# A decoder layer on one core: the projection stage of its mixer written out pass by pass, with other loads, statistics and transposes in its order

## The reference

```python
def _layernorm(x, axis=-1, eps=1e-05):
    m = jnp.mean(x, axis=axis, keepdims=True)
    v = jnp.var(x, axis=axis, keepdims=True)
    return (x - m) / jnp.sqrt(v + eps)
...
proj = jnp.einsum('btd,od->bto', x, W_in)
gate = proj[..., :DI]
value_raw = proj[..., DI:2 * DI]
params = proj[..., 2 * DI:].reshape(Bsz, Tlen, H, 2)
xp = jnp.pad(value_raw, ((0, 0), (K - 1, 0), (0, 0)))
conv = dw_bias + sum((xp[:, k:k + Tlen, :] * dw_weight[:, k] for k in range(K)))
value = jax.nn.silu(conv)
```

## Time and profile before

| What | us |
|---|---|
| median of 3 runs | 3239.29 |
| the profiled execution | 3251.73 |
| its span, first to last instruction | 3249.9 |
| projections in it, start to the first instruction of the mixer stage | 269.7 |
| of these, start to the first transpose | 29.7 |
| start of the first to start of the last pass's transposes (29.68 to 226.91) | 197.2 |

### The profile page before, as it was taken

One profiled execution on the slowest core, in us unless ns is written; L12 is line 12 of the kernel. 1 busy time (PEld: TensorE's weight loads), 2 busy tenths in 40 slices (PEclk: granted clock), 3 DMA queues, 4 the chain that ended last, 5 costly groups with the idle time before them and its releaser, 6 DMA issues. The chain is left out here.

```text
span 3249.9 us, 83432 instructions
## 1 busy us (share of the span) xinstructions
PE 2870.0 (88%) x34208; PEld 2165.1 (67%) x34208; DVE 2067.0 (64%) x7109; ACT 1299.5 (40%) x2250; POOL 287.0 (9%) x227
## 2 busy tenths in 40 slices
PE   5885699999999999999999998698887399999996
PEld 2444587788778877787887887333344166888885
DVE  5444999999999998899999998455452000111110
ACT  3443445454554455455544553133331021333332
POOL 0000000000000000000000000000004600434343
PEclk9887799999999999999999998689988599999998
DMA  6566323543354325433543242200062201777777
GB/s 225 160 160 177 93 83 82 131 106 89 76 131 105 96 69 131 105 90 74 132 107 105 71 118 72 75 1 1 1 238 91 104 14 56 202 206 203 205 203 214
DMA packets 249371, 373.92 MB, mean 115 GB/s; under 512 B 54203, under 2 KB 172108, under 8 KB 238156
## 3 DMA queue, kind: packets, MB, share of 16 engines
q1 hardware_dynamic: 226572, 340.18, 37.9%
q0 software_dynamic: 22464, 28.95, 4.4%
HBM read 269.18 MB, written 104.04 MB: 115 GB/s over the span
## 5 line engine op out<-in xcount | busy, mean ns | idle before, releaser
L603 PE MATMUL ring<-valt,wbc 128*128 128x256 f32 x4096 | 947.1, 388 | 28.8 <-DMA valt<-valt_scratch 28.1
L603 PEld LDWEIGHTS ring<-valt,wbc 128*128 128x128 f32 x4096 | 777.7, 194 | 166.7 <-issue 58.9
L756 ACT COPY bc<-ring 128x512 f32<-128x512 f32 x256 | 149.8, 585 | 746.6 <-PE ring L603 746.6
L916 DVE TENSOR_TENSOR uu<-phi,coef 128x64 f32<-128x64 f32 x2048 | 367.1, 223 | 2.1
L922 DVE TENSOR_TENSOR phi<-phi,uu 128x64 f32<-128x64 f32 x2048 | 367.3, 223 | 0.0
L2039 DVE TENSOR_SCALAR f_yr<-fp_y,f_meta 128x256 f32<-128x256 f32 x124 | 54.3, 480 | 415.8 <-PE fp_y L1856 415.8
L661 PE MATMUL yp<-bc,hpad 32*32 32x64 f32 x8192 | 260.4, 289 | 5.2 <-DVE hc L1024 5.0
L661 PEld LDWEIGHTS yp<-bc,hpad 32*32 32x32 f32 x8192 | 225.5, 122 | 51.3 <-issue 51.2
L1923 ACT ACTIVATE f_hT<-fp_h,f_b 128x256 f32<-128x256 f32 x248 | 117.6, 474 | 327.7 <-PE fp_h L1847 327.7
L1856 PE MATMUL fp_y<-f_w,f_hT 128*128 128x256 f32 x992 | 230.7, 386 | 7.9
L1723 POOL DMA_INDIRECT acc_scratch<-f_yr,f_meta x124 | 192.6, 1553 | 445.5 <-DVE f_yr L2039 304.7
(11 more groups left out here) (227 smaller groups left out, 4102.2 us busy)
## 6 DMA issues: line engine op xcount, KB each, us to landing
f_w<-in_W_dram SPq DMA_DIRECT2D x128, 512.0 KB
coef<-par_scratch SPq DMA_DIRECT2D x128, 256.0 KB
fb<-fac_scratch SPq DMA_DIRECT2D x256, 128.0 KB, 3.3
fc<-fac_scratch SPq DMA_DIRECT2D x256, 128.0 KB, 4.0
xg_scratch<-f_fill SPq DMA_DIRECT2D x16, 1032.0 KB, 17.3
f_xr<-xg_scratch SPq DMA_DIRECT2D x64, 258.0 KB
vtok_scratch<-p_vtok SPq DMA_DIRECT2D x32, 512.0 KB, 7.0
dub<-vtok_scratch SPq DMA_DIRECT2D x16, 1024.0 KB, 7.8
```

Of the source, the lines that this page charges most:

```text
L603: mm = pe.matmul(ring[:, p % 2, v * UT:(v + 1) * UT], wbc[:, k, g, first + v, :], valt[:, u % 2, k, :], start=(k == 0), stop=(k == 3))
L756: nc.scalar.copy(bc[:, gp, first:first + 2, i // 2, :], o).then_inc(bc_ready, 1)
L916: made[k] = mark(V.tensor_tensor(uu[:, k].rearrange("p i (g b) -> p i g b", b=B), phi[:, t, ::-1, k, :].rearrange("p i (g b) -> p i g b", ...
```

## The change

The stage does the same arithmetic on the same sizes; the loop of 4 rounds becomes straight-line code, pass by pass, with waits for constants, and the order changes:

- x is loaded by 8 DMAs of one pass each (512 KB). The first is issued ahead of the weights, the others behind them and ahead of `wbc`.
- VectorE takes the statistics of the first pass's 4 tiles alone, norms them, and then takes those of the other 28 tiles.
- TensorE's order in a pass is val, par, vt of the pass before, xT of the next pass, gate. `xnt` has two buffers.
- ScalarE takes the next pass's `xnt` and the last pass's `vtok` in the same order; the silu of `cv` stays behind that of the gates.
- VectorE norms the next pass's tiles ahead of a pass's convolution, and waits for the silu of the pass before ahead of writing `cv`.
- SP stores raw, vtok of the pass before, sg, valt. The `stored` semaphores are split by what they guard.

```diff
-PRING = [("xT", 0), ("xT", 1)] + [("val", m) for m in range(4)] + [("par",)]
-PRING += [("gate", m) for m in range(4)] + [("vt", b) for b in range(B)]
+def projection_order():
+
+    order = [("xT", 0, k) for k in range(2)]
+    for u in range(NPASS):
+        order += [("val", u, m) for m in range(4)] + [("par", u, 0)]
+        if u > 0:
+            order += [("vt", u - 1, b) for b in range(B)]
+        if u + 1 < NPASS:
+            order += [("xT", u + 1, k) for k in range(2)]
+        order += [("gate", u, m) for m in range(4)]
+    return order + [("vt", NPASS - 1, b) for b in range(B)]
+
+
+PRING = projection_order()
...
-        xt = sb("xt", [P, NT, DM])
-        bst = sb("bst", [P, NT, 6])
-        mv = sb("mv", [P, NT, 2])
-        std = sb("std", [P, NT])
-        rstd = sb("rstd", [P, NT])
+        xt = sb("xt", [P, NPASS, PA, DM])
+        bst = sb("bst", [P, NPASS, PA, 6])
+        mv = sb("mv", [P, NPASS, PA, 2])
+        std = sb("std", [P, NPASS, PA])
+        rstd = sb("rstd", [P, NPASS, PA])
...
-        xnt = sb("xnt", [P, 2, PT])
+        xnt = sb("xnt", [P, 2, 2, PT])
...
+            xv = x.rearrange("(a u p) m -> u p a m", a=PA, p=P)
+            sp.dma_start(xt[:, 0], xv[0]).then_inc(x_first, 16)
...
+            for u in range(1, NPASS):
+                sp.dma_start(xt[:, u], xv[u]).then_inc(x_in, 16)
...
-                sg_ready.wait(sp, u, 4)
+                    sp.dma_start(st["raw"][q, u // 2, :, (u % 2) * PT:(u % 2 + 1) * PT],
+                                 rawp[q * H:(q + 1) * H, :]).then_inc(raw_out, 16)
+
+            def store_sg(u):
+                sp.wait_ge(sg_ready, 4 * u + 4)
                 for v in range(2):
-                    sp.dma_start(st["sg"][2 * u + v], sg[:, par, :, v * UT:(v + 1) * UT]).then_inc(stored[par].sem, 16)
-
-                vtok_ready.wait(sp, u, 4 * B)
+                    sp.dma_start(st["sg"][2 * u + v], sg[:, u % 2, :, v * UT:(v + 1) * UT]).then_inc(sg_out[u % 2], 16)
+
+            def store_valt(u):
+                sp.wait_ge(valt_ready, 4 * u + 4)
+                for v in range(2):
+                    sp.dma_start(st["valt"][2 * u + v], valt[:, u % 2, :, v * UT:(v + 1) * UT]) \
+                        .then_inc(valt_out[u % 2], 16)
+
+            def store_vtok(u):
+                sp.wait_ge(vtok_ready, 2 * B * (u + 1))
                 for v in range(2):
                     for q in range(2):
-                        sp.dma_start(st["vtok"][2 * u + v, q], vtok[v * L:(v + 1) * L, par, :, q, :]) \
-                            .then_inc(stored[par].sem, 16)
-                valt_ready.wait(sp, u, 4)
...
+            for u in range(NPASS):
+                store_raw(u)
+                if u > 0:
+                    store_vtok(u - 1)
+                store_sg(u)
+                store_valt(u)
+            store_vtok(NPASS - 1)
...
-                xn_ready.wait(pe, u, 1)
-
-                vtok_ready.wait(pe, u, 2 * B)
...
+            normed_turned(0)
+            for u in range(NPASS):
+                values(u)
+                if u > 0:
+                    values_turned(u - 1)
+                if u + 1 < NPASS:
+                    normed_turned(u + 1)
+                gates(u)
+            values_turned(NPASS - 1)
...
-            nc.scalar.activation(std[:], mv[:, :, 1], ACT.Sqrt, bias=epsln[:, 0:1]).then_inc(std_ready, 1)
-            act.wait_ge(w_loaded, 16 * NW)
...
+            nc.scalar.activation(std[:, 0], mv[:, 0, :, 1], ACT.Sqrt, bias=epsln[:, 0:1]).then_inc(std_ready, 1)
...
+            def values(u):
+                if u >= 2:
+                    act.wait_ge(conv_ready, 4 * (u - 1) + 4)
...
+                if u > 0:
+                    act.wait_ge(raw_out, 32 * u)
...
+            normed_turned(0)
+            for u in range(NPASS):
+                values(u)
+                if u == 0:
+                    act.wait_ge(stats_ready, 2)
+                    nc.scalar.activation(std[:, 1:].rearrange("p u a -> p (u a)"),
+                                         mv[:, 1:, :, 1].rearrange("p u a -> p (u a)"), ACT.Sqrt,
+                                         bias=epsln[:, 0:1]).then_inc(std_ready, 1)
+                else:
+                    values_turned(u - 1)
+                if u + 1 < NPASS:
+                    normed_turned(u + 1)
+                gates(u)
+                convolved(u)
+            values_turned(NPASS - 1)
...
-            dve.wait_ge(x_in, 16)
-            for n in range(NT):
-                ins = V.bn_stats(bst[:, n, :], xt[:, n, :])
-            ins.then_inc(step, 1)
-            dve.wait_ge(step, 1)
-            for n in range(NT):
-                ins = V.bn_aggr(mv[:, n, :], bst[:, n, :])
-            ins.then_inc(stats_ready, 1)
-            dve.wait_ge(std_ready, 1)
-            V.reciprocal(rstd[:], std[:]).then_inc(step, 1)
-            dve.wait_ge(step, 2)
-            dve.wait_ge(w_loaded, 16 * NW)
...
+            def statistics(u0, u1, k):
+                for u in range(u0, u1):
+                    for a in range(PA):
+                        ins = V.bn_stats(bst[:, u, a, :], xt[:, u, a, :])
+                link(ins)
+                for u in range(u0, u1):
+                    for a in range(PA):
+                        ins = V.bn_aggr(mv[:, u, a, :], bst[:, u, a, :])
+                ins.then_inc(stats_ready, 1)
+                dve.wait_ge(std_ready, k)
+                link(V.reciprocal(rstd[:, u0:u1], std[:, u0:u1]))
...
+            def normed(u):
+                if u >= 2:
+                    dve.wait_ge(xnt_ready, 2 * (u - 1))
...
+                    if u > 0:
+                        dve.wait_ge(valt_ready, 4 * (u - 1) + k + 1)
...
+            dve.wait_ge(x_first, 16)
+            statistics(0, 1, 1)
+            normed(0)
+            dve.wait_ge(x_in, 16 * (NPASS - 1))
+            statistics(1, NPASS, 2)
+            dve.wait_ge(w_loaded, 16 * NW)
+            for u in range(NPASS):
+                if u + 1 < NPASS:
+                    normed(u + 1)
+                convolution(u)
```

More of the change, by code:

```diff
@@ L121, in projections @@
         std_ready = sem("std_ready")
[L122 to L132, removed]
-        step = sem("step")
[L135 to L144, removed]
+        ring_full = sem("ring_full")
+        xn_ready = sem("xn_ready")
+        xnt_ready = sem("xnt_ready")
+        vraw_ready = sem("vraw_ready")
+        raw_ready = sem("raw_ready")
+        raw_out = sem("raw_out")
+        sg_ready = sem("sg_ready")
+        conv_ready = sem("conv_ready")
+        valt_ready = sem("valt_ready")
+        vtok_ready = sem("vtok_ready")
+        sg_out = [sem(f"sg_out{i}") for i in range(2)]
+        vtok_out = [sem(f"vtok_out{i}") for i in range(2)]
+        valt_out = [sem(f"valt_out{i}") for i in range(2)]
+        step = sem("step")
         block = ctx.enter_context(nc.Block())
@@ L178, in _ @@
-            passes(sp, body)
-            for s in stored:
-                sp.wait_ge(s.sem, 128 * (NPASS // 2) + 128)
-            sp.wait_ge(raw_out.sem, 32 * NPASS + 32)
+                        sp.dma_start(st["vtok"][2 * u + v, q], vtok[v * L:(v + 1) * L, u % 2, :, q, :]) \
+                            .then_inc(vtok_out[u % 2], 16)
+            for u in range(NPASS):
[4 more added lines that the diff above has]
+                store_valt(u)
@@ L214, in body, with gates @@
-                o = put(("par",))
+                    mm.then_inc(ring_full, 1)
+                o = put(("par", u, 0))
                 for k in range(2):
-                    mm = pe.matmul(o[0:2 * H, :], win[:, k, 2 * DI:2 * DI + 2 * H], xnt[:, k, :],
+                    mm = pe.matmul(o[0:2 * H, :], win[:, k, 2 * DI:2 * DI + 2 * H], xnt[:, u % 2, k, :],
                                    start=(k == 0), stop=(k == 1))
-                full(mm)
+                mm.then_inc(ring_full, 1)
+            def gates(u):
@@ L219, in body @@
                 for m in range(4):
-                    o = put(("gate", m))
+                    o = put(("gate", u, m))
                     for k in range(2):
-                        mm = pe.matmul(o, win[:, k, m * P:(m + 1) * P], xnt[:, k, :], start=(k == 0), stop=(k == 1))
-                    full(mm)
-                valt_ready.wait(pe, u, 4)
+                        mm = pe.matmul(o, win[:, k, m * P:(m + 1) * P], xnt[:, u % 2, k, :],
+                                       start=(k == 0), stop=(k == 1))
@@ L232, in _ @@
-            passes(pe, body)
+                                          valt[:, u % 2, k, :].rearrange("p (t b) -> p t b", b=B)[:, :, b], ident[:])
+                    mm.then_inc(ring_full, 1)
+            normed_turned(0)
[7 more added lines that the diff above has]
+            values_turned(NPASS - 1)
         @block.scalar
@@ L235, in _ @@
         def _(act):
+            act.wait_ge(init_ready, 1)
             act.wait_ge(stats_ready, 1)
[L237 to L269 removed]
@@ new lines, in values, with gates @@
+            def values(u):
```

(21 more changed lines are left out.)

135 lines of the change are left out of this document (66 added, 69 removed).

## The result

The changed kernel takes 3169.4 us (median of 4 runs, 3152.0 to 3176.0) against 3238.8 (4 runs, 3238.3 to 3249.2): ratio 0.9775, 95% interval 0.9750 to 0.9799. The forecast was 3163, its own range 3156 to 3171. The profiled execution took 3166.4 us, with a span of 3164.5; before, 3249.9.

The account below looks back on a forecast made before the run. TensorE was taken as nearest to the bound, its work lengthened by gaps and a falling clock. Gains of 19.8 (head) + 56.1 (middle) - 0.3 (tail) = 75.6 us gave 3163 us, own range 3156 to 3171, overall range 3150 to 3188.

Parts of the forecast that it names:

- The pass: Middle passes: every operand is there in time, so TensorE's own work sets 18.7 us a pass; 56.1 us gained.
- The head: Stage start: first transpose at 13.8, val of pass 1 at 41.5 against 61.27; 19.8 us gained.
- The new wait: Pass 0: TensorE waits 3.5 us for the second tile, as the second square root stands behind ScalarE's params copy.
- The third rival: Head gains half: weights or other tiles late, or square root's place costs more; +10 us, 3173; chance 0.08.
- The tail: Last pass: the queue of transfers decides, ending 40.4 us after val against 40.1 before; 0.3 us lost.
- The sum of the stage: Whole first stage: head 19.8, middle 56.1, tail -0.3, together 75.6 us gained.
- The first rival, a falling clock: Passes: the clock falls without a gap, as transposes leave the array little to do; 23 us, 3186; chance 0.13.
- The second, transfers: Passes and tail: transfers cost 20% more and take over, pass 19.7, tail 3 longer; +9 us, 3172; chance 0.12.
- The fourth, stalls for code: Passes: engines stall for straight-line code; a loss from two 4.92 us stalls a pass on (3242); chance 0.03.
- The whole time: Whole kernel: the stage's gain taken off the median, 3239.3 - 76, gives 3163 us.

Follow-up runs that it names:

- e9: Changed kernel with the second pass's load, statistics and norming also ahead of the other tiles', and the `vtok` fill on GpSimd; stage ended at 185.4 us (changed kernel 194.8).
- e7: Changed kernel with `valt` stored a second time to a spare tensor, 1 MB more a pass; stage ended at 204.7 us.
- e6: Changed kernel with each of vt's transposes done four times, 64 in place of 16, same results; stage ended at 233.5 us.
- e8: Changed kernel with `vtok` stored by 2 DMAs from 128 partitions instead of 4 from 64, scratch laid out to suit; stage ended at 184.5 us.
- e11: Changed kernel with two passes at the head, `vtok` stored from 128 partitions, and the last pass's `cv` and gate silus in turns; 3161.4 us, ratio 0.9734.
- e1: Kernel before the change with its loop of 4 rounds written out and nothing else changed; ratio 0.9998, stage ended at 264.1 us.
- e4: Changed kernel with vt put back behind its own pass's gates, xT staying amid the products; stage ended at 219.8 us.
- e5: Changed kernel with xT put back behind the gates, vt staying amid the products; stage ended at 201.5 us.
- e2: Changed kernel with the old head: x by one DMA, all statistics first, one square root; 3180.0 us, ratio 0.9800.

## Why the prediction was right

**The pass: right.** 18.7 was forecast, 18.59 measured, from val(1) to val(7) 111.5 us against 112.2. The terms held as well: vt 2.19 and xT 1.04 for 2.1 and 1.0, VectorE 12.9 for 13.0, ScalarE 11.4 for 11.9, transfers 16.2 for 16.4. No wait of TensorE ended with ScalarE after pass 1 but the last. One price in the range didn't fit its own source: 16 transposes at 0.21 instead of 0.13 us are 1.3 us a pass, not 0.5. It didn't matter, as they took 0.14.

**The head: right in its mechanism, 2.3 us too hopeful.** Val(1) was to come at 41.5, between 40.0 and 43.2, and came at 43.76, outside that range; the gain was 17.5, not 19.8. I had counted the square root's table load at nothing. It ran at the start before; now it stands behind the same wait as the square root, and runs on the path (the first row is before, the second after):

```profile
0.73 1.28 ACT L237 ACT_TABLE_LOAD   x1 [0.73 <-PEq L2103]
...
11.41 1.28 ACT L274 ACT_TABLE_LOAD   x1 [11.41 <-DVE p_mv L359]
```

That is the first transpose's 14.78 for 13.8. The other tiles were seen at 19.99 instead of 16, and so the statistics, not ScalarE's order, set the second square root:

```profile
3.31 10.12 SPq L160 DMA_DIRECT2D p_xt<-in_x_dram  x7
```

```profile
19.99 9.24 DVE L355 BATCH_NORM_STATS2 p_bst<-p_xt 128x6 f32<-128x256 f32 x28 [5.35 <-DMA p_xt<-in_x_dram]
...
31.26 0.32 ACT L326 ACTIVATE p_std<-p_mv,p_epsln 128x28 f32<-128x28 f32 x1 [1.94 <-DVE p_mv L359]
```

SP needed 10.12 us to issue the seven loads. The new wait was 4.70 us, not 3.5, and the clock then stood at 0.50 for the start of the gates (8.75 us, inside the 6.9 to 9.1 given). The third rival named this place, and its sign, a gap over 4 us, did show; it priced it at 10 us, and it was 2.3. e9 shows that this wait and the fill were what held the head: without them val(1) comes at 33.4.

The same head didn't always run alike. In the second trace of the changed kernel val(1) came at 43.63 and in e7 at 42.98, again with xT at 1.97; in e6 and e8 it came at 40.28 and 40.46. There val of pass 0 took 10.0 and 10.2 us instead of 8.6 to 9.0, the wait behind it was only 2.67 us, and xT and the gates then ran at full speed (1.09 and 7.03). And in these two the square root did wait for ScalarE's copy of the params, as the prediction had it (e6):

```profile
30.68 0.33 DVE L362 RECIPROCAL p_rstd<-p_std 128x28 f32<-128x28 f32 x1 [2.10 <-ACT p_std L326]
```

So which of the two ends last isn't fixed, and from xT to val(1) it takes 10.35 us or 7.80, as the clock falls or holds.

**The tail: right.** 40.4 was forecast from val(7), 39.5 measured. That stores set it is shown by e8 (wide stores, -7.0) and e11 (the last silus earlier, -0.1).

**The sum of the stage: partly luck.** 75.6 was forecast and 74.9 measured, but the head's 2.3 us too few were mostly made good by 0.7 in the passes and 0.9 in the tail.

**The first rival, a falling clock: refuted.** The passes run at 1.00, and e6 holds it through 64 transposes in a row. The Trainium skill's rule ("TensorE: Matmul & The Clock Gate", section "Part 4: PE-mode transpose") that transposes don't count as busy for the clock gate is not borne out by this case, whose transposes are of float32: had the clock fallen at them, the passes would have lost up to 3.3 us each by the prediction's price, and they lost none.

**The second, transfers: not here, but near.** With 2.3 us a pass to spare, nothing was lost. e7 puts 2.8 us more in, and then the transfers fall behind by 1.4 us a pass, which is 1 us more than the sum says of the changed kernel's 16.2 us and the added 2.8. That surcharge is smaller than the 20% of this rival: 20.02 for 19.0, 5%. The DMA engines stand at 0.98 in it, so 2 of the 5% are idle time between stores; the rest stays unexplained.

**The fourth, stalls for code: refuted** by e1 (ratio 0.9998), and by passes that are alike to 0.01 us.

**The whole time.** The forecast from the median was 3163, the stage's miss of 0.7 makes it 3164, and 3169 was measured. What is left lies behind the stage, where the two profiled executions differ by another 10.5 us (85.4 between the spans, 74.9 in the stage). Cross-attention took 306.8 us in the profiled run and 318.5 before, at clocks of 0.95 and 0.89 for a stretch of 200 us inside it (the first row is after, the second before):

```profile
1994.80:2194.80 200.00, 174.38 (x1282) 75.41 (x1286) 120.40 (x190) 72.03 (x135) 0.00 (x0) 0.95 0.05 16
```

```profile
2069.70:2269.70 200.00, 176.00 (x1238) 76.73 (x1238) 112.55 (x183) 68.80 (x128) 0.00 (x0) 0.89 0.04 13
```

It isn't the change: the same unchanged code took 314.8 in the second profile of the changed kernel, 306.7 in e8, 320.8 in e11. All stages behind took 2961 to 2985 us over the 14 profiled executions, a spread that covers the 6 us missed. Why the clock differs there from one execution to the next stays open.

## What to carry to other kernels

A wait of TensorE on another engine's last step goes away when its next independent products are put between that step and its consumer; the two groups to move need not both be moved to get most of it (vt alone gave 42 of the 54 us in the passes). Once the bound engine is full, look at the ends. The first pass's statistics alone were worth 10.0 us in the stage, those of the second with the fill on GpSimd another 9.4, and the layout of the stores 7.0. The second moved group, beside vt, is worth 11.7 in the passes (123.2 - 111.5). And judge a stage by the trace: here 16 us in one stage didn't show against the scatter of the others.

## What the runs showed of the hardware

- A single gap of 2.76 us ahead of transposes cost TensorE its clock in four of seven passes of e4, and in the last pass of five of the eight executions that have it ahead of 16 transposes (vt of 3.13 to 3.69 us for 2.19). One of 1.66 to 1.71 us ahead of products never did (e5).
- Transposes of 128x128 float32, one after another, hold the clock at 1.00 for 8 us and take 0.12 us each (e6).
- Stores of `vtok` from 64 partitions ran at about 210 GB/s, from 128 at 375 to 387 (e8); those of `sg` and `valt`, from 128, at 337 to 374. The Trainium skill says in "SBUF — State Buffer", section "Door 1: The DMA port swizzle", that partitions 0 to 63 reach only 8 of 16 ports, with 196 GB/s measured at 1 MB against 328 from all 128; the trace agrees in kind, for stores.
- ScalarE's table load can stand behind the wait of the activation that needs it, and then adds its 1.28 us to the path: so in the changed kernel (11.41) and e2 (27.11), whose square root stands behind two waits. Before, with one wait in the code, the load ran at 0.73, ahead of it. That the number of waits decides this is not shown.
- Stores queued without a pause, with the DMA engines at 0.98, took 5% longer than the sum of their times (e7: 20.02 us for 19.0).
